# Position rows read into the tokens' place, table rows added by the gather: the first batch of a language-model tower

## What is computed

```python
h = sum over 8 shards of W[shard][clip(x - start, 0, 1574)]
h = h + shards * bias + pos_emb          # pos_emb: 512 x 1024
h = h + attention(layernorm(h))          # 32 heads, 8 key/value heads, causal
h = h + ffn(layernorm(h))                # per-head MLP on permuted features
```

## Time and profile before

| | us |
|---|---|
| median of 3 runs | 2604.17 |
| lowest, highest | 2603.53, 2606.53 |
| the profiled execution, its own time | 2604.64 |
| its span | 2602.7 |

### The profile page before, as it was taken

The page is one execution under the profiler, slowest core; times in us unless marked ns, Lnnn a source line. Parts: engine busy times, 40 slices in busy tenths (PEclk is TensorE's granted clock), DMA queues, the critical chain, the costliest instruction groups (busy, mean ns, idle before and its releaser), DMA issues.

```text
span 2602.7 us, 35197 instructions
## 1 busy us (share of the span) xinstructions
PE 2584.7 (99%) x12982; PEld 2111.9 (81%) x12982; DVE 1194.3 (46%) x3147; ACT 989.3 (38%) x2612; POOL 318.4 (12%) x266
## 2 busy tenths in 40 slices
PE   8999999999999999999999999999999999999998
PEld 6888888888878877888887887788888778878884
DVE  5444444554444434455444443445445344434444
ACT  5544444454343333224333334322433333332232
POOL 5233334333000000100000000010000000000002
PEclk9999999999999999999999999999999999999999
DMA  5556668655544444644443443463444444434432
GB/s 168 182 196 223 212 218 276 219 202 205 181 135 161 146 140 133 211 146 139 146 158 133 161 144 137 146 209 137 146 150 146 143 142 161 146 133 144 142 128 97
DMA packets 135190, 425.67 MB, mean 164 GB/s; under 512 B 15918, under 2 KB 15918, under 8 KB 135022
## 3 DMA queue, kind: packets, MB, share of 16 engines
q1 hardware_dynamic: 127488, 398.00, 44.2%
q0 software_dynamic: 7424, 25.17, 3.4%
q10 hardware_dynamic: 110, 0.26, 0.0%
HBM read 322.71 MB, written 100.66 MB: 163 GB/s over the span
## 4 chain that ended last, share of the span: by engine, by line
PE 97%; DMA 1%; ACT 0%; DVE 0%; POOL 0%; issue 0%; ACTq 0%; POOLq 0%; SPq 0%; DVEq 0%
PE fb L556 22%; PE fb L558 22%; PE fb L557 22%; PE tp L591 6%; PE pv L556 3%; PE sc L556 3%; PE sc L557 3%; PE sc L558 3%; PE pv L558 3%; PE pv L557 3%; PE sc L643 2%; PE fb L652 2%; PE sc L582 1%; PE pv L605 1%; PE pv L637 1%; PE fb L637 1%
## 5 line engine op out<-in xcount | busy, mean ns | idle before, releaser
L556 PE MATMUL fb<-xn_hi,w_both 128*128 128x512 f32 x1504 | 596.0, 396 | 0.0
L558 PE MATMUL fb<-xn_hi,w_both 128*128 128x512 f32 x1504 | 587.5, 391 | 0.0
L557 PE MATMUL fb<-xn_lo,w_both 128*128 128x512 f32 x1504 | 586.2, 390 | 0.0
L556 PE MATMUL fb<-at_hi,w_both 128*128 128x512 f32 x992 | 394.0, 397 | 0.0
L558 PE MATMUL fb<-at_hi,w_both 128*128 128x512 f32 x992 | 387.7, 391 | 0.0
L557 PE MATMUL fb<-at_lo,w_both 128*128 128x512 f32 x992 | 386.3, 389 | 0.0
L829 ACT ACTIVATE prob<-sc,neg_max 128x128 f32<-128x128 f32 (+3 forms) x512 | 263.0, 526 | 286.4 <-DVE neg_max L960 286.4
L556 PEld LDWEIGHTS fb<-xn_hi,w_both 128*128 128x128 f32 x1504 | 282.4, 188 | 75.4 <-issue 18.8
L1015 DVE TENSOR_TENSOR hacc<-hacc,fb 128x512 f32<-128x512 f32 x256 | 175.8, 687 | 349.3 <-PE fb L558 348.9
L558 PEld LDWEIGHTS fb<-xn_hi,w_both 128*128 128x128 f32 x1504 | 282.3, 188 | 60.3
L557 PEld LDWEIGHTS fb<-xn_lo,w_both 128*128 128x128 f32 x1504 | 282.7, 188 | 57.2
(11 more groups left out here) (211 smaller groups left out, 3466.6 us busy)
## 6 DMA issues: line engine op xcount, KB each, us to landing
w_both<-qkv_halves SPq DMA_DIRECT2D x268, 512.0 KB, 3.6
w_both<-dense_halves SPq DMA_DIRECT2D x192, 512.0 KB, 3.8
qkv_halves<-w_both SPq DMA_DIRECT2D x96, 512.0 KB, 3.8
dense_halves<-w_both SPq DMA_DIRECT2D x64, 512.0 KB, 3.4
w_raw<-in_w_qkv SPq DMA_DIRECT2D x116, 256.0 KB, 4.1
w_raw<-in_w_dense SPq DMA_DIRECT2D x64, 256.0 KB, 3.8
h_rows<-hacc SPq DMA_DIRECT2D x32, 256.0 KB, 2.3
h_tok<-in_pos SPq DMA_DIRECT2D x12, 512.0 KB, 7.3
```

The lines of the kernel that those rows point to most:

```text
L556: pe.matmul(dst, a_hi, b_hi, start=first, stop=False)
L557: pe.matmul(dst, a_hi, b_lo, start=False, stop=False)
L558: return pe.matmul(dst, a_lo, b_hi, start=False, stop=last)
```

## The change

In the first batch, too, the position rows are read straight to `h_tok`, and the gather adds the table rows to them. The steps `J0` to `J3`, the buffer `first_pos` and the semaphore `h_placed` go; TensorE waits for the gather itself. POOL keeps the wait for gather c-2 and waits for the chunk's position rows besides.

```diff
-START = ("A G0 G1 G2 G3 w0 w1 w2 J0 J1 B0 B1 La0 B2 Lb0 B3 La1 J2 X0 X1 w3 Lb1 C0 B4 B5 La2 J3 X2 X3 Lb2 C1 w4 B6 B7 La3 "
+START = ("A G0 G1 G2 G3 w0 w1 w2 B0 B1 La0 B2 Lb0 B3 La1 X0 X1 w3 Lb1 C0 B4 B5 La2 X2 X3 Lb2 C1 w4 B6 B7 La3 "
          "X4 X5 Lb3 a0 C2 a1 X6 X7 C3 a2 a3 Q0 K Q1 V")
...
-        with ExitStack() as own:
-            at_hi = sb("at_hi", [P, HQ, S], F32R, own)
-            at_lo = sb("at_lo", [P, HQ, S], F32R, own)
-        first_pos = sb("first_pos", [P, TT, E], F32)
+        at_hi = sb("at_hi", [P, HQ, S], F32R)
+        at_lo = sb("at_lo", [P, HQ, S], F32R)
...
-        h_placed = sem("h_placed")
...
             def first_positions(c):
-                sp.dma_start(first_pos[:, c, :], pos[c * P:(c + 1) * P, :]).then_inc(pos_in[c], 16)
+                sp.dma_start(h_tok[:, c, :], pos[c * P:(c + 1) * P, :]).then_inc(pos_in[c], 16)
...
                     if s.b == 0:
-                        pe.wait_ge(h_placed, c + 1)
+                        pe.wait_ge(gathered[c], 16)
                         mm = pe.matmul(dst, ident[:, :], h_tok[:, c, half * S:(half + 1) * S], start=False, stop=True)
...
-                elif s.kind == "J":
-                    dve.wait_ge(pos_in[s.i], 16)
-                    dve.wait_ge(gathered[s.i], 16)
-                    dve.tensor_tensor(h_tok[:, s.i, :], h_tok[:, s.i, :], first_pos[:, s.i, :], ALU.add)\
-                       .then_inc(h_placed, 1)
...
                     if s.b == 0:
                         if s.i > 1:
                             pool.wait_ge(gathered[s.i - 2], 16)
-                        pool.indirect_dma_start(out=h_tok[:, s.i, :], out_offset=None, in_=table, in_offset=token)\
-                            .then_inc(gathered[s.i], 16)
-                    else:
-                        pool.wait_ge(pos_in[s.i], 16 * s.b + 16)
-                        pool.indirect_dma_start(out=h_tok[:, s.i, :], out_offset=None, in_=table, in_offset=token,
-                                                compute_op=ALU.add).then_inc(gathered[s.i], 16)
+                    pool.wait_ge(pos_in[s.i], 16 * s.b + 16)
+                    pool.indirect_dma_start(out=h_tok[:, s.i, :], out_offset=None, in_=table, in_offset=token,
+                                            compute_op=ALU.add).then_inc(gathered[s.i], 16)
```

More of the change, by code:

```diff
@@ L97, in unit @@
             out.append(Step(kind, b, 0, i))
-        elif kind in ("A", "G", "J", "B", "C", "La", "Lb", "X", "a", "w"):
+        elif kind in ("A", "G", "B", "C", "La", "Lb", "X", "a", "w"):
             out.append(Step(kind, b + 1, 0, i))
```

## The result

The changed kernel takes 2611.43 us (median of 9 runs, 2610.32 to 2612.60) against 2604.17 us of the kernel before: 7.26 us more, a ratio of 1.0028 with a 95% interval of 1.0020 to 1.0037. A second set of nine runs gave 2610.99 against 2604.18, ratio 1.0027 (1.0017 to 1.0037). So it is slower, by a little more than what can be told from no change. The forecast was 2609.9, in a range of 2605.0 to 2615.5, with 0.59 for slower.

A forecast was written before the change was run, and what follows sets the result against it. TensorE, busy 99% of the span, bounds the kernel, so only a delay of its first projection counts. X4 moves from 27.33 to 33.0, and 2604.17 + 5.7 = 2609.9 us; range 2605.0 to 2615.5.

The forecast's parts named there:

- Chunk 2 sets X4: Start of the kernel: chunk 2 arrives at 27.2, so TensorE's step X4 starts at 33.0 instead of 27.33, 5.7 us later.
- parts 2 and 3: Gathers waiting for positions, chunk 2 arriving at 27.2; then the way from arrival to X4 at 33.0.
- its tail of 5.8: From chunk 2's arrival to X4: 2.3 us until its statistics steps end, then 3.5 us to X4.
- the chain: First batch: positions 0, gather 0 and gather 2 stand in a row, chunk 2 arriving at 27.2.
- Part 1: Four VectorE additions of 1.23 or 1.21 us removed; only the first lies bare on its chunk's way, 1.23 us once.
- TensorE or ScalarE is as late: Claim that removing the additions after the first gains nothing; ScalarE idles 1.44 us for a weight tile at 20.84.
- the clock at nothing: The sum counted no loss from TensorE falling to 1.2 GHz in its 7 us idle gap before chunk 0.
- that rival: TensorE's clock falls and slows the tail of the start: 1 to 5 us more, taken as 3, 2612.9; chance 0.15.
- Short gathers: Rival: mean length of gathers 0 and 2 between 7.0 and 8.9; at 7.7 shift 2.8 us, 2607.0, no measurable change; chance 0.37.
- The other side: Rival: gathers so short that removed additions count, start faster below 6.3 us length; 3.7 needed for 5.2 us; chance 0.04.
- the clock at its bound: Low clock until a0: B4 pushed about 1.2 us, up to 4 us more after; the range's upper end, 2615.5.

The follow-up runs named there:

- the half change: The kernel before with the change made for chunks 2 and 3 alone, chunks 0 and 1 keeping plain gather and VectorE's addition: 2606.59 us (+2.41), ratio 1.0010.

## Why the prediction was right, and where it wasn't

**Right: the place and the sign.** All of the loss lies before a0 and reaches the end nearly whole; the additions taken from VectorE won nothing that shows. Gather 0 at 8.08 (forecast 8.14), its length 9.5 (9.5), chunk 0 at 17.6 (17.6), chunk 1 at 20.9 (19.9), X4 at 32.99 (33.0). The low parts of the weights moved behind gather 3, to 22.58 (22.3), and stayed hidden.

**Wrong: "Chunk 2 sets X4" in parts 2 and 3.** X4 agreed to 0.01 us by luck, because errors of opposite sign met, and in an execution that was shorter than most. I gave gather 2 8.8 us and it took 6.2, so chunk 2 was whole at 24.5 and not at 27.2; with its tail of 5.8 X4 would have come at 30.3. What I left out is that TensorE and ScalarE can't take chunk 2 before they have done chunk 0 and 1: their own work from chunk 0's last pass to X4 is 11.44 us, from chunk 1's 8.96. By chunk 1's relay at the full clock X4 would have come at 32.1 (20.9 + 11.2), and the low clock adds the other 0.9. In the kernel before these relays were covered by a wait for weight tile 2, as its chain of waits shows:

```profile
13.02 7.80 DMA w_raw<-in_w_qkv
...
21.69 1.45 ACT prob L820 x2
```

The test that separates the two is the chain: cutting it won nothing (+7.59), and bringing chunk 0 back alone won nothing either (+7.54), since chunk 1 came at 21.2 all the same and X4 then follows it.

**Part 1's reading of the additions was half right.** They were worth nothing in this change. But "TensorE or ScalarE is as late" holds only while ScalarE waits for weight tile 2: with that wait gone, the additions of chunks 1 and 3 are on the path.

**Wrong: the clock at nothing.** The granted clock fell to 0.50 in the wait for gather 0. I had that rival with "most of it inside the wait for chunk 2"; but chunk 0's passes lie on the way themselves. The price differs from execution to execution. By chunk 1's landing + 11.2 us, its relay at the full clock, the low clock cost an estimated 0.9 us in the changed kernel's first trace, 1.7 in its second (21.65 + 11.2 against 34.55), 2.5 without the wait for gather c-2 (21.54 + 11.2 against 35.19) and 0.1 with plain gathers (19.19 + 11.2 against 30.51). Filling the wait gives 1.4 to 1.8 us back by medians, 0.4 to 1.3 by median spans. The forecast, 5.7 us, lacked 1.1 and 1.6 to the 6.8 and 7.3 measured: the clock is of that size, but no run shows that it is all of it. The warning of the Trainium skill (TensorE: Matmul & The Clock Gate, HAM oscillation) that an idle TensorE drops to 1.2 GHz holds in this case's rows.

**The parts of the loss,** from medians against the kernel before: the wait for the positions with plain gathers and a busy TensorE, 3.4 us; adding on top of it, 5.4 - 3.4 = 2.0 us; the clock, 1.4 to 1.8 us. (By median spans: 3.8, 2.4 and 0.4 to 1.3.) They are read off a ladder of kernels and not independent: adding without the wait costs 4.3 us by another way, through gather 2 and VectorE's additions. The 95% interval of each kernel's ratio is about 2.5 us wide, so the single parts are rough.

**The other rivals.** Short gathers: two of the four were (6.2 and 6.7), and it was of no use, as the two that count were 9.5 and 10.0. The other side, a chain so short that the start gains, was never near. The 3.2 us that the fit of the Trainium skill (DMA: Bandwidth & Descriptors, Anatomy of one DMA) gives for 512 KB, an estimate, is below every gather seen here, the shortest plain one being 4.2. One small sum of the forecast is off: the clock at its bound, 1.2 + 4 us, gives 2615.1 and not 2615.5.

Still open: how X4 comes about in the shorter executions of the half change, how long the low clock lasts in the median execution of each kernel, and what fills the 1.8 to 3.6 us outside the span.

## What to carry to other kernels

To let a DMA add on top of another DMA's result puts the two in a row and lengthens the second; what it saves on a vector engine counts only if that engine was the last to be waited for. Where a pipeline is filled chunk by chunk, reckon from each chunk's arrival the work that all engines still have to do in their fixed order, and take the latest, before naming the last arrival as the bound. Work that is off the path today can stand right behind what is on it: here VectorE's additions came to bound the start as soon as a weight tile no longer did. Where one profiled execution is compared with another, see first where each lies among the spans of its kernel. And a wait of several microseconds on TensorE in a start has a second price, that of the passes behind it.

## What was not expected of the hardware

An adding gather of 512 KB is 1.8 to 2.7 us longer than a plain one in the same place (9.5 against 6.8 for gather 0 and 6.7 against 4.2 for gather 3; with TensorE kept busy, 9.4 against 7.6 and 6.7 against 4.9), more than the 1.0 us that I had worked out from the queues' shares. And its length differs even more by what runs beside it: 6.2 to 6.7 us once the position reads are in, 9.4 to 10.7 among them in the changed kernel and its variants that start it near 8 us, 8.4 to 9.0 in the two kernels that have a part of the change, 8.4 to 10.5 where it is issued without waiting for positions. TensorE ended waits of 4.35, 4.91, 6.72, 7.29, 8.33 and 8.46 us with passes at the low level (2.08 us a pair), and waits of 2.42, 1.74 and 1.50 us with passes at the high one (1.12 or 1.13).
